# A two-layer attention and mixture-of-experts kernel: the attention's front two steps shorter, layer 1's list built with exchanged operands, some VectorE work on Pool

## The reference

```python
xn = _layernorm(x, axis=-1)
x = x + _L0_attn_ref(xn, ...) + _L0_ffn_ref(xn, ...)
xn = _layernorm(x, axis=-1)
x = x + _L1_attn_ref(xn, ...) + _L1_ffn_ref(xn, ...)
```

```python
q = _l2norm(q) * q_scale
k = _l2norm(k) * k_scale
sim = jnp.einsum('bhid,bhjd->bhij', q, k) * ATTN_SCALE
sim = sim + dist[None, None] * slopes[None, :, None, None]
attn = jax.nn.softmax(sim, axis=-1)
out = jnp.einsum('bhij,bhjd->bhid', attn, v)
```

## Time and profile before

| | us |
|---|---|
| median of 3 runs | 706.15 |
| lowest and highest | 699.28, 707.43 |
| the profiled execution | 700.29 |
| its span in the trace | 698.5 |
| TensorE busy | 609.3 |
| ScalarE busy | 433.4 |
| VectorE busy | 428.5 |
| Pool busy | 333.7 |

### The profile page before, as it was taken

The page is one execution under the profiler, slowest core; times in us unless marked ns, Lnnn a source line. Parts: engine busy times, 40 slices in busy tenths (PEclk is TensorE's granted clock), DMA queues, the critical chain, the costliest instruction groups (busy, mean ns, idle before and its releaser), DMA issues.

```text
span 698.5 us, 13423 instructions
## 1 busy us (share of the span) xinstructions
PE 609.3 (87%) x3791; PEld 478.7 (69%) x3791; DVE 428.5 (61%) x1542; ACT 433.4 (62%) x1197; POOL 333.7 (48%) x290
## 2 busy tenths in 40 slices
PE   2447989976899898889999999999999999998897
PEld 1445778764667776667777777777777777766566
DVE  5764546456777666767656655555565566576643
ACT  3802867425876768655467777777776777766452
POOL 3528752225878534233144444554455433788600
PEclk9998999988899989979989999999999999999789
DMA  9501222400111013000000100010001100021100
GB/s 307 178 15 47 76 77 62 162 20 1 31 31 31 2 34 89 1 0 2 1 20 23 29 24 16 24 31 24 17 23 33 23 9 12 25 61 50 46 1 9
DMA packets 26326, 29.13 MB, mean 42 GB/s; under 512 B 3920, under 2 KB 22384, under 8 KB 25744
## 3 DMA queue, kind: packets, MB, share of 16 engines
q1 hardware_dynamic: 21680, 18.89, 8.5%
q0 software_dynamic: 4576, 9.38, 5.7%
HBM read 19.94 MB, written 8.32 MB: 40 GB/s over the span
## 4 chain that ended last, share of the span: by engine, by line
PE 66%; DVE 14%; issue 7%; POOL 6%; ACT 3%; DMA 2%; another core or an unknown queue 1%; SPq 0%; DVEq 0%; ACTq 0%; POOLq 0%
PE b_upB L1771 10%; PE b_last L1786 9%; PE b_upB L1758 5%; PE b_last L1651 4%; PE b_rest L1835 4%; PE b_rest L1626 4%; PE b_rest L1585 3%; POOL rn L554 2%; PE b_upA L1450 2%; PE b_rest L1806 2%; PE b_upA L1704 2%; PE b_last L1450 2%; PE b_upA L1451 2%; PE b_upA L1452 2%; POOL taken L601 2%
## 5 line engine op out<-in xcount | busy, mean ns | idle before, releaser
L847 ACT ACTIVATE prb<-prb,mneg 128x130 f32<-128x130 f32 (+1 forms) x256 | 115.1, 451 | 110.1 <-DVE mneg L1393 103.7
L1393 DVE CUSTOM_DVE_ANT_0 prb<-b_upB,bias 128x130 f32<-128x130 f32 (+1 forms) x256 | 84.3, 357 | 149.9 <-PE b_upB L1771 141.4
L554 POOL TENSOR_TENSOR rn<-ss,halves 128x8 f32<-128x8 f32 x64 | 108.1, 1691 | 132.2 <-DVE ss L1331 131.6
L495 POOL DMA_INDIRECT moe_buf<-normal_rows,source x79 | 79.2, 1003 | 123.5 <-PE b_rest L1738 74.9
L1771 PE MATMUL b_upB<-qkT 64*128 64x258 f32 (+1 forms) x512 | 99.5, 389 | 14.8 <-DVE mneg L1393 9.0
L1786 PEld LDWEIGHTS b_last<-v,prT_all 128*128 128x128 f32 x768 | 103.6, 198 | 11.8 <-DVE qs_all L1379 4.9
L1786 PE MATMUL b_last<-v,prT_all 128*128 128x64 f32 x768 | 104.4, 274 | 2.9 <-DVE qs_all L1379 2.9
L1771 PEld LDWEIGHTS b_upB<-qkT 64*128 64x128 f32 x512 | 50.1, 193 | 44.8 <-issue 22.0
L856 ACT ACTIVATE prT_all<-b_rest 128x512 f32<-128x512 f32 (+1 forms) x128 | 61.2, 478 | 7.4 <-PE b_rest L1835 6.6
L1835 PE MATMUL b_rest<-cst,prb 128*128 128x128 f32 x384 | 64.6, 278 | 0.3 <-issue 0.3
L1835 PEld LDWEIGHTS b_rest<-cst,prb 128*128 128x128 f32 x384 | 48.7, 153 | 20.4 <-issue 19.9
(11 more groups left out here) (321 smaller groups left out, 1308.3 us busy)
## 6 DMA issues: line engine op xcount, KB each, us to landing
expert_rows<-moe_buf SPq DMA_DIRECT2D x20, 128.0 KB
expert_rows<-moe_buf SPq DMA_DIRECT2D x39, 64.0 KB
bias<-w_up SPq DMA_DIRECT2D x1, 2048.0 KB, 9.6
down<-w_dn SPq DMA_DIRECT2D x2, 1024.0 KB, 10.1
moe_buf<-w_up SPq DMA_DIRECT2D x4, 512.0 KB, 4.0
moe_buf<-normal_rows,source POOLq DMA_INDIRECT x79
qk<-x SPq DMA_DIRECT2D x8, 128.0 KB, 4.1
v<-w_qk SPq DMA_DIRECT2D x1, 1024.0 KB, 11.9
```

Source lines behind the costliest of these rows:

```text
L495: nc.gpsimd.indirect_dma_start(out=room, out_offset=None, in_=normal_rows[layer], in_offset=bass.IndirectOffsetOnAxis(ap=source[layer][:, ...
L554: nc.gpsimd.tensor_tensor(rn[hs], ss[hs], halves[:], ALU.pow).then_inc(pool_root, 1)
L847: nc.scalar.activation(prb[k % 3][:, i, 0:n], prb[k % 3][:, i, 0:n], ACT.Exp, scale=-1.0, bias=mneg[:, qt, h:h + 1], accum_out=lsum[:, qt, ...
L1393: nc.vector.tensor_tensor_reduce(prb[k % 3][:, i, 0:n], b_sim[i][:, 0:n], bias[:, h, KEYS - n:KEYS], 1.0, FMAX, ALU.add, ALU.min, mneg[:, ...
```

## The change

- The front: projection, sum, root and product of a piece come two steps later against the scores, `T1_AT` too; the turn stays. A turn stands behind two later projections instead of three, and the waits are set to that.
- Batch 0: ticks 7 to 12 of the mixing move from steps -15 to -10 to steps -11 to -6, batch 0's rows are turned ahead of tick 7, and on VectorE its normalization and rho stand in step -15, behind tick 6.
- The list: the products of layer 1 take the numbers as the stationary and the lane marks as the moving operand. The result (40 x 128, `b_lanes`) is copied to SBUF in step 44 and turned by TensorE in step 45; `source` is copied in step 45, as are the shares computed; gathers start in step 46. The first tile is in step 48, the last in 98, the last gathers start in 105.
- From VectorE to Pool: batch 3's products (`ON_DVE`), the normalization of batches 4 to 7 and the low part of the four weight quarters.

```diff
@@ -210,6 +210,7 @@
         dist = prb[0][:, 0]
+        lanes_room = fill[0:SLOTS].rearrange("p e i -> p (e i)")
         nk_sq = sq[0:NULL * H1, 0:2 * DH1].rearrange("p (a d) -> p a d", a=2)
...
@@ -238,7 +239,8 @@
         mix_bank = [b_gate, b_up, *b_sim, b_pv, b_y, b_gate, b_up]
-        b_source = [b_prT[:, 64:64 + SLOTS], b_gate[:, 256:256 + SLOTS]]
+        b_source = [b_prT[:, 64:64 + SLOTS], b_gate[:, 256 + P:256 + P + SLOTS]]
+        b_lanes = b_gate[0:SLOTS, 256:256 + P]
         b_tile = b_y[:, 0:P]
...
@@ -332,10 +335,10 @@
-        PROJ_AT, SUM_AT, ROOT_AT, UNIT_AT, TURN_AT, V_AT = -11, -10, -9, -8, -4, 2
-        T1_AT = STEPS - 13
-        TILE0 = 3 * STEPS - 1
+        PROJ_AT, SUM_AT, ROOT_AT, UNIT_AT, TURN_AT, V_AT = -9, -8, -7, -6, -4, 2
+        T1_AT = STEPS - 11
+        TILE0 = 3 * STEPS
         TILES1 = 2 * TILES + E - 1
...
@@ -357,7 +360,7 @@
-        ON_DVE = (0, 3)
+        ON_DVE = (0,)
         FIRST = lambda n: [f"max{n}", f"hit{n}", f"named{n}", f"least{n}", f"pick{n}"]
...
@@ -372,7 +375,8 @@
         ROUTE0 = 2 * STEPS - 4
-        MIX_AHEAD, MIX_STEP = 6, -STEPS
+        MIX_AHEAD = 6
+        MIX_AT = [-STEPS, -11, -10, -9, -8, -7, -6]
         SOURCE0 = 2 * STEPS + 6
...
@@ -542,6 +546,19 @@
+            def x1_normal(b):
+                pool.wait_ge(x1_r, 4)
+                pool.wait_ge(xn_set, b)
+                for i in range(T * b, T * b + T):
+                    ins = nc.gpsimd.tensor_scalar(xf_all[:, i], acc_all[:, i], rowmv[:, i, 0:1], rowr[:, 0, i:i + 1], ALU.subtract, ALU.mult)
+                ins.then_inc(xn_set, 1)
+            def split_up(c):
+                pool.wait_ge(up_hi[1], c + 1)
+                nc.gpsimd.tensor_tensor(quarter(up_l, c), raw_up(1, c), quarter(up_h, c).bitcast(F32), ALU.subtract).then_inc(up_lo[1], 1)
...
@@ -570,13 +587,17 @@
                     row_roots(3)
+                if 22 <= s < 26:
+                    x1_normal(s - 18)
             def tile_rows(s):
+                if s - 1 in SPLIT_AT:
+                    split_up(SPLIT_AT.index(s - 1))
                 if s == SOURCE0 + 1:
                     pool.wait_ge(*ROUTED("marked", 1))
                     nc.gpsimd.tensor_tensor(numbered[1], named, token_names(), ALU.mult).then_inc(named_set, 1)
-                if s == SOURCE0 + 7:
+                if s == SOURCE0 + 8:
                     pool.wait_ge(kept[1], 16 * B)
...
@@ -744,8 +765,8 @@
             def late_mixing(s):
-                if MIX_STEP <= s < MIX_STEP + B + 5 - MIX_AHEAD:
-                    mixing(MIX_AHEAD + s - MIX_STEP)
+                if s in MIX_AT:
+                    mixing(MIX_AHEAD + MIX_AT.index(s))
...
@@ -1030,7 +1047,10 @@
-                dve.wait_ge(lanes_read, (layer + 1) * CHUNKS)
+                if layer:
+                    dve.wait_ge(lanes_turned, 1)
+                else:
+                    dve.wait_ge(lanes_read, CHUNKS)
                 nc.vector.tensor_copy(source[layer][:], b_source[layer]).then_inc(*routes[layer]("source"))
...
@@ -1195,6 +1215,8 @@
+                if b == 0:
+                    dve.wait_ge(x1_r, 1)
                 for i in range(T * b, T * b + T):
...
@@ -1218,8 +1240,9 @@
                     x1_variances(0)
+                if s == 1 - STEPS:
+                    x1_normal(0)
                     x1_rhos(0)
-                    x1_normal(0)
                 if s == -5:
...
@@ -1234,8 +1257,6 @@
                     x1_normal(2 + (s > 11))
-                if 22 <= s < 26:
-                    x1_normal(s - 18)
...
@@ -1308,10 +1329,11 @@
                     slots(1)
+                    dve.wait_ge(lanes_read, 2 * CHUNKS)
+                    nc.vector.tensor_copy(lanes_room, b_lanes).then_inc(lanes_copied, 1)
+                if s == SOURCE0 + 7:
                     sources(1)
                     route1_part(15)
-                if s - 1 in SPLIT_AT:
-                    split_up(1, SPLIT_AT.index(s - 1))
...
@@ -1523,9 +1545,15 @@
                     k = CHUNK * q + c
-                    ins = nc.tensor.matmul(b_source[layer], lane_room(layer, q)[:, c], numbered[layer][:, k], start=(k == 0), stop=(k == 2 * TILES - 1),
-                                           skip_group_check=True)
+                    hot, number = lane_room(layer, q)[:, c], numbered[layer][:, k]
+                    ins = nc.tensor.matmul(b_lanes if layer else b_source[0], number if layer else hot, hot if layer else number,
+                                           start=(k == 0), stop=(k == 2 * TILES - 1), skip_group_check=True)
                 ins.then_inc(lanes_read, 1)
+            def turn_sources():
+                pe.wait_ge(lanes_copied, 1)
+                nc.tensor.transpose(b_source[1], lanes_room, ident[0:SLOTS, 0:SLOTS]).then_inc(lanes_turned, 1)
...
@@ -1634,15 +1662,15 @@
                         pe.wait_ge(wqk_lo, 2)
-                    if m > 3:
-                        pe.wait_ge(act_turn, m - 3)
+                    if m > 2:
+                        pe.wait_ge(act_turn, m - 2)
                     if n == 0:
                         pe.wait_ge(dve_xa_l, b + 1)
                     project_qk(b_front, t, w * HD1 + g * 512).then_inc(pe_proj, 1)
                 for m in piece_at(s, TURN_AT):
                     w, t, g = piece_of(m % 8)
-                    pe.wait_ge(act_proj, min(m + 4, 8 * B))
+                    pe.wait_ge(act_proj, min(m + 3, 8 * B))
                     if m:
...
@@ -1681,6 +1709,8 @@
                     sources(1, q)
+                if s == SOURCE0 + 7:
+                    turn_sources()
                 if 12 in route_at(s):
```

25 lines of the change are left out of this document (11 added, 14 removed).

## The result

The changed kernel takes 678.38 us (median of 4 runs, 674.23 to 688.04), the kernel before 703.76 (4 runs, 699.28 to 707.43). The ratio is 0.9622, with a 95% interval of 0.9532 to 0.9713: faster by 3.8%.

A forecast was written before the change was run, and what follows sets the result against it. TensorE was taken as the bound, busy 609.3 of 698.5 us, with waits and low clock costing about equally. Terms -3.0 - 8.8 + 1.5 + 0.5 - 2.0 gave -11.8 us: 694 us against the 706.15 median, range 683 to 707.

The forecast's parts named there:

- Term 1: Start: batch 0's turn behind one mixing tick and the shorter front bring first scores to about 170.3 us; -3.0 us.
- third rival: Start: first scores come no earlier because Pool's roots set the turns; term 1 is 0, total 697 us; chance 0.07.
- Term 2: Steps 36 and 44: less VectorE work and the list's later step shrink two waits and end their low clock; -8.8 us.
- more of them go: More low-clock stretches vanish, also those of the end and of 246 or 171; another 7 us, 687 us; chance 0.15.
- Term 3: Work moved to Pool: its time is mostly covered, but it blocks VectorE's small copies; +1.5 us.
- fourth rival: Steps 20 to 26: Pool becomes the bound, with 21.5 us queued against 23; 713 us; chance 0.10.
- Term 4: Layer 1's list: exchanged operands stream 128 columns instead of 40, plus an extra turn; +0.5 us (-0.8 to +1.1).
- Term 5: End, from step 104: Pool sets the pace and the last row update moves one step nearer the end; -2.0 us.

The follow-up runs named there:

- The added lump: Changed kernel plus three useless VectorE reductions of 512 columns at the end of steps 14, 22, 30 and 42; 0.9788 of the kernel before.
- the variant with batch 7 alone: Changed kernel with the unit products of batch 7, the last batch, on VectorE instead of Pool; 0.9607 of the kernel before.
- The kernel with the step alone: Changed kernel with the list's old operands, no copy or turn, but all its new steps kept; 0.9662 of the kernel before.
- the best variant: Changed kernel with the list's old operands, its later steps kept, and batch 7's unit products on VectorE; 663.49 us, 0.9566 of the kernel before.
- the filled kernel before: Kernel before plus 18 useless TensorE products of 512 columns in six steps ahead of the first scores; 1.0026 of the kernel before.

## Why the prediction was off

*Where the gain is.* The reading that half of the looseness is clock, and that waits of some 2 us bring it down, was right. It is shown by the filled waits, which move the fall ahead of the first scores in all three kernels that have them, and by the lost clock over the runs. The added lump points the same way but isn't clear of noise by itself. The gain is 20.9 us clock and 5.7 us rest on the chip where both kernels ran most often.

*Term 1* (-3.0 us, first scores 170.3). The steps at tick 6 went as written: VectorE's tick 6 at 145.68, a wait of 1.31 where 1.3 was said, full clock behind it, first scores 169.59, and the low clock ahead of them stays (6.8 us lost, 5.1 before). The lead in step 8 is 6.6 us. The term was 3.3 us too small at step 16: the lead at the first scores is 4.8 where I had 4.1, and the 1.1 us for the projection that moves behind them doesn't show. The parts of the sum differ, though. The term gave the order 3.9 us and the front 0.25 (1.65 for a projection less 1.4 of waiting). Counted from the last product ahead of tick 6, the order makes up the whole lead (24.6 us with the long front, where the kernel before has 30.0), and the short front adds nothing. So the third rival's premise held, that the front brings the first scores no earlier, and the term was right by the order.

*Term 2* (-8.8 us) is **the step that failed, by its size**, and with it the assumption that only the two falls would go whose waits these edits shorten. They went, 6.8 us. But the falls at 246 and 297 went too, another 6.8. The prediction had the first as a bound (-15) and not in the term, and said that the change leaves the wait on ScalarE ahead of it. It does not: 1.56 us before is 0.98 now, and so it is with the short front alone (0.98; with the list alone 1.57), which puts it down to the front. The other wait stands as it was, 1.69 us for `pnT`. From step 16 to step 52 the lead grows by 14.9 us, Pool's price included, where terms 2 to 4 said 6.8. The tally shows why a profile misleads here: a wait of 1.3 to 1.75 us has a fall with it about once in three (and the one for `pnT` 12 times in 18), so which falls one profile holds is partly a draw, and a change that shortens waits ahead of one alters what is drawn behind those that stay. The rival "more of them go" had 0.15, at 7 us; it came, at 11.1 (6.8 in these stages, 4.3 at the end). That isn't the luck of one profile, since the means over the runs on the fourth chip say the same (20.9 us of lost clock, where the two profiles differ by 19.7). But the profiled run is a lucky one of its four: on the chip of the result they lost 14.1 to 26.1 us, and it lost the least.

*Term 3* (Pool's price, +1.5 us). Pool is full in steps 20 to 26, and nobody waits for it beyond 0.2 us; the fourth rival did not come:

```profile
234.00:257.00 23.00, 20.55 (x141) 15.52 (x140) 15.51 (x58) 18.37 (x53) 22.29 (x18) 1.00 0.23 65
...
L560 POOL TENSOR_TENSOR up_l<-moe_buf,up_h x4: 2368/2382/2418, 237.5 to 270.6; 128x1024 fp32r<-128x1024 f32 x4
...
238.56 1.37 DVE L1448 COPY pn<-prb 128x12 f32<-128x12 f32 x1
...
242.01 0.63 DVE L1448 COPY pn<-prb 128x12 f32<-128x12 f32 x1
```

A split is 2.38 us (estimated 2.1). Of VectorE's six small copies in these 23 us one is held for 1.37 us beside a split, and the others take 0.17 to 0.63, against a usual 0.17. So the long ones are blocked for about what the overlap allows, as the Trainium skill has it ("SBUF — State Buffer", "Who interferes with whom"), but few instructions fall into such an overlap. Over the whole profile that copy grew by 1.2 us in 128. VectorE gave up 13.1 us of instructions and is left with 8.0 less in their sum, so those that stayed grew by some 5 us, where the term had 4. What part of it reached TensorE isn't shown; alone, the whole move gave 3.0 us of rest.

*Term 4* (exchanged list, +0.5 us). One of the list's 64 products is 273 ns (before 283) and its weight load 117 (before 192):

```profile
L1549 PEld LDWEIGHTS b_upA<-th,moe_buf x64: 112/117/117, 309.5 to 326.8; 128*40 128x40 f32 x64
L1549 PE MATMUL b_upA<-th,moe_buf x64: 272/273/303, 309.5 to 326.9; 128*40 128x128 f32 x64
```

The loads ran beside other products, and no run shows a gain from it: with the old operands and batch 7 on VectorE the kernel is the best of all. Whether the 0.7% are batch 7's alone isn't settled: the variant with batch 7 alone stood at 0.9607 and the one with old operands alone at 0.9662 on the third chip, which speaks for batch 7, with intervals that overlap. The kernel with the step alone (0.9662) keeps what the kernel with the list undone (0.9764) loses, so what helps in this part of the change is, as far as two chips can be compared, the step: it takes the sources and shares out of step 44 and with them the 2.04 us wait.

*Term 5* (-2.0 us, 0 to -7). From step 96 to 132 the lead grows by 5.3 us, while the low clock in that stretch costs 6.8 us less (1.7 where it was 8.5). So all of it is clock, and the rest of this stage has got no shorter. Behind step 132 another 0.9 us is lost, with the new low clock behind 667. Against it stands what I missed: in these steps Pool's unit product comes just ahead of its turn, and TensorE waits 3.08 us for it. The prediction had named Pool as the pace of this stage, but not that the shorter front leaves a piece there less slack, so that the pace shows up as a wait. With batch 7 on VectorE that wait is gone.

*The sum and the chances.* From profile to profile the time fell by 26.1 us where the sum said 11.8. Of the 14.3 us between them, 3.3 lie ahead of step 16, 8.1 in the stages of term 2, and 2.9 behind. The range's lower end, 683, came from adding one rival to the terms. The parts hardly add (2.1% alone, 5.9% taken out), and a range built on a sum could not hold that.

## What to carry to other kernels

When a kernel's TensorE falls to its lower clock in several places, price the falls together: count the waits by size, and count what a fall costs (4.2 us here, in the mean) times the share of such waits that have one, instead of asking only which single wait the change removes. Parts of a change that each shorten waits can be worth little alone and much together, so try the whole before a part is thrown out for being neutral. Work moved to an engine that is half idle on average is to be placed by that engine's queue at the step: Pool took four splits, eight normalizations and eight products without being waited for in the stages with room, and one of its products where it paces the last steps kept TensorE waiting 3 us.

## What the runs showed of the hardware

- The 57 falls in the middle of the 18 profiles cost 1.7 to 8.5 us each, 3.4 (25 of them) or 5.1 (19) as a rule, and 4.2 in the mean. The waits with them are mostly of 1.3 to 3.6 us. So the loss behind a wait can be larger than the wait.
- Waits of 1.75 us and more had the lower clock (a granted clock of 0.5, 1.2 GHz) begin in them or within 3 us behind them in 22 of 27 cases, those of 1.3 to 1.75 us in 26 of 84. The page "TensorE: Matmul & The Clock Gate" of the Trainium skill ("A second HAM failure mode") tells of a kernel whose small idle times between groups of products made the clock swing. The profiles here agree, and the tally gives that a size.
- The same program lost between 24.0 and 47.9 us of clock in 11 runs on one chip. Its time varied from 685.9 to 705.84 us in them. On another chip the best variant lost 12.5 to 14.6 in 6 runs and varied by 3 us, where the kernel before lost 27.4 to 46.3 and varied by 15.7 in 17. That fits fewer waits that may or may not have a fall, but wasn't tested by itself.
- Useless products that fill the waits ahead of the scores keep the clock up there (1.00 from 160 to 176 us in the filled kernel before) and cost as much as they bring: 2.8 us less lost clock against 3.2 us more rest in the kernel before, and no gain in the changed one.
